# Attention sums taken through DRAM into the row order of the output projection, in an fp32 transformer block on one core

## The chip, the core and the metric

The kernel runs on one core of a Trainium2 chip. Its engines are TensorE (PE in the profile; PEld are its weight loads), VectorE (DVE), ScalarE (ACT), GpSimd (POOL) and SyncE (SP), which here only issues transfers. Each engine works through its own instructions in order; semaphores hold one engine back until another has come far enough. The metric is the time of one execution on the device in microseconds (us). Before the change it is 394.41 us, the median of three runs (393.88 to 394.71).

## The reference

One pre-norm block on x of 2048 tokens by 256, all in fp32: causal attention with 16 heads of 16, then a dense layer with 8 LoRA experts of rank 16, of which each token takes its best two.

```python
h = layernorm(x)
Q, K, V = (heads(h @ W.T) for W in (q_proj, k_proj, v_proj))
p = softmax(causal(Q @ K.T / sqrt(16)))
x = x + merge(p @ V) @ o_proj.T
n = layernorm(x)
logits = n @ gate_w.T + gate_b
best two experts, gates = softmax of their logits
x = x + n @ W.T + b + sum(gate * lora_B[e] @ (lora_A[e] @ n))
```

## The kernel before

The tokens are 16 tiles of 128 and 4 chunks of 512 (4 tiles each). The heads are taken in 4 quads, and two quads are a half (m = 0 or 1). Attention runs with keys on the rows: scores of a block of 128 keys against up to 512 queries go to PSUM (L696), ScalarE takes the exponential of two heads at once (L814), VectorE clears the later keys of diagonal blocks (L1010, the masks), and a product with v_aug adds the block to acc (L713). v_aug holds, for each head, 16 columns of v and 16 of ones, so acc has for each head of a quad 16 rows of numerators and 16 rows that all hold the denominator. When a quad of a chunk is complete, keep_sums copies acc to SBUF (L1015).

The order is set by a table in steps. A step is two units of scores (two exponentials), at most one piece, and the value products of units some steps back. A unit is one bank pair of scores; there are three such pairs, so scores run ahead of the exponentials by little. Chunk c begins at step 0, 10, 36 and 78; the last unit is in step 135. Pieces before attention (turn_x, project_qk, project_v, norms) prepare the next chunk: they stand in steps 0 to 23 and 36 to 49. Pieces after it finish tiles 0 to 11: seven a tile, turn_sums, turn_back, o, turn_y, ffn, turn_gated, lora. All of them use one PSUM bank, aux, so a piece waits until the one before it has been read (bank_read). The four tiles of the last chunk follow when attention is over, in the tail, in an order of their own (TAIL_ORDER).

Per tile, turn_sums (L623) turns the four quads' sums to tokens on the rows, VectorE takes the reciprocal of the 16 denominators (L1020) and multiplies (L1022), turn_back (L630) turns the 256 columns back, VectorE copies them (attn_t, L1027), o multiplies by wo (L637), VectorE adds x (L1033), takes statistics (L1035 to L1040), GpSimd makes the power (L1211), VectorE normalises (yln, L1044). Then turn_y, the copy yT, ffn (L651), the routing (L1055 to L1070), the gates (L1075 to L1089; they wait for GpSimd's exp_gap, L1216), turn_gated (L657), the copy gatedT (L1094), lora (L662), and the result (L1104). The normalisation and the gates are put one step later than their piece, ahead of all else of that step. In the tail ScalarE makes the copies attn_t, yT and gatedT.

SyncE stores the 16-bit parts of q and k of each projected tile to DRAM (L481 to L486) and, when a chunk's four tiles are there, reads them back in the order of the stacks (L455, L464), 16 transfers for a chunk.

## Time and profile before

| | |
|---|---|
| median of 3 runs | 394.41 us |
| profiled execution | 393.18 us, of which the span is 391.4 |
| TensorE busy | 354.2 us (90%) |
| ScalarE busy | 279.5 us (71%) |
| VectorE busy | 209.7 us (54%) |
| GpSimd busy | 47.8 us (12%) |

The span begins with the first instruction and ends with the last; 1.8 us of the execution lie outside it. Busy shares are means over stages that differ, so they don't tell what a stage waits for. A wait in brackets in a timeline is the idle time of the engine before the row, with what ended it.

### The profile page before, as it was taken

What the parts mean: (1) busy time and instruction counts of PE and PEld (TensorE: products, weight loads), DVE (VectorE), ACT (ScalarE), POOL (GpSimd) and SP (SyncE); (2) the same over time, 40 slices, a digit from 0 to 9 for tenths busy, and PEclk for the clock granted to TensorE, in tenths of its full rate; (3) what the DMA queues carried; (4) which work ended last, traced back from release to release, by engine and by line L of the source; (5) the groups of instructions that cost most, each with busy time, mean ns of one, the idle gap of its engine ahead of it and who ended that gap; (6) DMA issues with size and microseconds to landing.
All of it is one profiled execution on the core that took longest, in us unless ns stands there. A gap on an engine that the chain in (4) does not pass through costs nothing.

```text
span 391.4 us, 6977 instructions
## 1 busy us (share of the span) xinstructions
PE 354.2 (90%) x2558; PEld 138.0 (35%) x2558; DVE 209.7 (54%) x711; ACT 279.5 (71%) x317; POOL 47.8 (12%) x75
## 2 busy tenths in 40 slices
PE   8967978899998999999999999998999899799874
PEld 3545524354333444423323233232322323222542
DVE  4555558455755654555447464546346543600785
ACT  2544438677887877888788887888878688799311
POOL 5011000000011100011121111211112111100040
PEclk9997969999999999999999999999999999999997
DMA  6479444222450022271000000000000000000001
GB/s 202 139 224 315 116 131 141 55 55 54 124 148 13 2 54 75 62 214 44 13 2 13 3 13 16 3 13 2 13 16 0 16 0 15 13 2 3 0 3 55
DMA packets 29380, 23.31 MB, mean 60 GB/s; under 512 B 15392, under 2 KB 25888, under 8 KB 29344
## 3 DMA queue, kind: packets, MB, share of 16 engines
q1 hardware_dynamic: 29344, 22.84, 19.8%
q8 instruction: 21, 0.34, 0.4%
q14 instruction: 15, 0.12, 0.1%
HBM read 12.35 MB, written 10.49 MB: 58 GB/s over the span
## 4 chain that ended last, share of the span: by engine, by line
PE 63%; DVE 20%; ACT 7%; issue 6%; POOL 2%; DMA 1%; DVEq 0%; ACTq 0%
PE acc L713 23%; PE scores L696 12%; PE aux L596 7%; ACT probs L814 6%; PE aux L651 5%; PE aux L637 3%; DVE probs L1010 2%; PE aux L662 2%; PE aux L602 2%; PE aux L623 1%; DVE ffn L1055 1%; POOL exp_gap L1216 1%; PE aux L644 1%; DVE gates L1083 1%; DVE parts L954 1%
## 5 line engine op out<-in xcount | busy, mean ns | idle before, releaser
L814 ACT ACTIVATE probs<-scores 128x1024 f32<-128x1024 f32 x272 | 260.2, 1032 | 69.1 <-PE scores L696 59.1
L713 PE MATMUL acc<-probs,v_aug 128*32 128x512 f32 (+3 forms) x1280 | 145.4, 545 | 1.3 <-ACT probs L814 0.9
L696 PE MATMUL scores<-q_stack,k_stack 64*128 64x512 f16 (+3 forms) x640 | 86.5, 352 | 3.7 <-ACT probs L814 2.0
L696 PEld LDWEIGHTS scores<-q_stack,k_stack 64*128 64x128 f16 x640 | 21.1, 94 | 103.6 <-ACT probs L814 80.3
L1010 DVE TENSOR_TENSOR probs<-probs,mask_sb 128x512 f32<-128x512 f32 (+1 forms) x80 | 44.2, 577 | 22.5 <-ACT probs L814 22.0
L713 PEld LDWEIGHTS acc<-probs,v_aug 128*32 128x32 f32 x1280 | 30.8, 110 | 49.8 <-issue 29.7
L596 PE MATMUL aux<-xT,wqkv_sb 128*128 128x128 f32 x192 | 26.3, 294 | 1.0 <-DVE xT L941 1.0
L596 PEld LDWEIGHTS aux<-xT,wqkv_sb 128*128 128x128 f32 x192 | 24.0, 203 | 5.4 <-issue 3.1
L952 DVE CAST parts<-qk 128x512 f16<-128x512 f32 x12 | 5.1, 427 | 36.5 <-ACT qk L806 36.5
L1207 POOL TENSOR_TENSOR rstd<-ve,minus_half 128x1 f32<-128x1 f32 x12 | 7.3, 608 | 101.6 <-DVE ve L932 101.6
L1211 POOL TENSOR_TENSOR rstd<-ve,minus_half 128x1 f32<-128x1 f32 x12 | 6.6, 549 | 103.8 <-DVE ve L1040 103.8
L651 PE MATMUL aux<-wffn_sb,yT 128*128 128x392 f32 x48 | 19.0, 518 | 0.0
L1033 DVE TENSOR_TENSOR y<-aux,x_sb 128x256 f32<-128x256 f32 x12 | 5.1, 424 | 23.9 <-PE aux L637 23.9
L1216 POOL TENSOR_TENSOR exp_gap<-euler,top_gap 128x1 f32<-128x1 f32 x12 | 6.6, 550 | 86.3 <-DVE top_gap L1068 86.3
L1055 DVE COPY ffn<-aux 128x392 f32<-128x392 f32 x12 | 6.8, 567 | 19.0 <-PE aux L651 19.0
L1015 DVE COPY sums<-acc 128x512 f32<-128x512 f32 x16 | 11.0, 686 | 7.0 <-PE acc L713 7.0
L602 PE MATMUL aux<-wqkv_sb,xT 128*128 128x256 f32 x48 | 13.6, 405 | 1.2 <-ACT qk L806 1.0
L1044 DVE TENSOR_SCALAR yln<-y,mv,rstd 128x256 f32<-128x256 f32 x12 | 9.7, 811 | 8.0 <-POOL rstd L1211 8.0
L637 PE MATMUL aux<-wo_sb,attn_t 128*128 128x256 f32 x48 | 13.6, 405 | 0.0
L1104 DVE TENSOR_TENSOR result<-aux,yb 128x256 f32<-128x256 f32 x12 | 5.1, 425 | 14.7 <-PE aux L662 14.7
L806 ACT COPY qk<-aux 128x512 f32<-128x512 f32 x12 | 7.0, 585 | 8.1 <-PE aux L596 5.6
L657 PE MATMUL aux<-ident_sb,gated 128*128 128x128 f32 x12 | 3.9, 327 | 9.0 <-DVE attn_t L1027 8.1
(146 smaller groups left out, 323.0 us busy)
## 6 DMA issues: line engine op xcount, KB each, us to landing
q_stack<-q_dram SPq DMA_DIRECT2D x32, 128.0 KB, 2.8
k_stack<-k_dram SPq DMA_DIRECT2D x32, 128.0 KB, 2.8
qk_dram<-qk SPq DMA_DIRECT2D x12, 256.0 KB, 2.5
x_sb<-x SPq DMA_DIRECT2D x3, 512.0 KB, 6.4
q_dram<-parts SPq DMA_DIRECT2D x12, 128.0 KB, 2.0
k_dram<-parts SPq DMA_DIRECT2D x48, 32.0 KB, 1.9
out<-result SPq DMA_DIRECT2D x12, 128.0 KB, 1.7
qk_dram<-probs SPq DMA_DIRECT2D x4, 256.0 KB, 3.3
```

The source lines that it names most:

```text
L596: m = pe.matmul(aux[:, n * P:(n + 1) * P], wqkv_sb[:, k, col:col + P], xT[:, k, :], start=(k == 0), stop=(k == KH - 1))
L602: m = pe.matmul(aux[:, 0:D], xT[:, k, :], wqkv_sb[:, k, 2 * D:3 * D], start=(k == 0), stop=(k == KH - 1))
L637: m = pe.matmul(w.bank[:, 0:D], w.attn_t[:, k, :], wo_sb[:, k, :], start=(k == 0), stop=(k == KH - 1))
L651: m = pe.matmul(w.bank[:, 0:FFN], w.yT[:, k, :], wffn_sb[:, k, :], start=(k == 0), stop=(k == KH - 1), skip_group_check=True)
L696: m = pe.matmul(scores[u % BANKS][:, j, col:col + n], k_stack[row:row + STACK, kb // TPC, 2 * i + p, kb % TPC * P:(kb % TPC + 1) * P], q_s ...
L713: m = pe.matmul(acc[32 * hp:32 * hp + 32, lo:CHUNK], v_aug[:, kb, QUAD * i + hp, :], probs[:, u % PROBS, hp % 2, col:col + CHUNK - lo], st ...
L814: act.activation(probs[:, u % PROBS], scores[u % BANKS][:], ACT.Exp, scale=EXP_SCALE).then_inc(exp_done, 1)
L1010: dve.tensor_tensor(tile, tile, mask, ALU.min).then_inc(causal_done, 1)
L1015: dve.tensor_copy(sums[:, c % 3, i, :], acc[:]).then_inc(acc_read, 1)
L1044: dve.tensor_scalar(w.yln, w.y, w.mv2[:, 0:1], w.rstd2, ALU.subtract, ALU.mult).then_inc(yln_ready, 1)
L1055: dve.tensor_copy(w.ffn, w.bank[:, 0:FFN]).then_inc(ffn_ready, 1)
L1216: pool.tensor_tensor(w.exp_gap, euler[:], w.top_gap, ALU.pow).then_inc(gap_exp, 1)
```

## The change

Each half of a chunk's sums (two quads, 128 rows by 2 x 512) is stored to DRAM when it is complete, one step later read back with four transfers into `attn`, whose row order is that of the input of o: one plane of numerators, one of denominators, 128 rows by 512 tokens each. wo's rows are permuted on the host to fit. From the fourth step after the store on, VectorE divides one tile (128 x 128) in each of four steps, a reciprocal and a product. o of tiles 0 to 11 takes its input there; turn_sums, turn_back and the copy attn_t go. Their tiles have five pieces. `sums` has one buffer instead of three.

In the tail only the last half (quads 2 and 3 of chunk 3) is still turned, divided and turned back. The first half of the tail's o and the residual x (a product of the identity with x) are put into the banks ahead of the last value products; ScalarE copies the finished sum out (keep_y), and VectorE's addition of x goes.

```diff
-POST_PIECES = ("turn_sums", "turn_back", "o", "turn_y", "ffn", "turn_gated", "lora")
+POST_PIECES = ("o", "turn_y", "ffn", "turn_gated", "lora")
+DIVIDE_LAG = 4
+            for t in range(TPC):
+                at.setdefault(s + DIVIDE_LAG + t, []).append((c, m, t))
...
+            def store_sums(c, m):
+                sp.wait_ge(acc_read, NQUAD * c + 2 * m + 2)
+                sp.dma_start(sums_dram[c, m], sums[:, 2 * m:2 * m + 2, :]).then_inc(sums_out[m], 16)
+
+            def load_sums(c, m):
+                sp.wait_ge(sums_out[m], 16 * (c + 1))
+                if c >= 2:
+                    sp.wait_ge(o_psum, TPC * (c - 1))
+                rows = sums_dram[c, m].rearrange("(h n d) q t -> n q d h t", h=QUAD, n=2)
+                for n in range(2):
+                    for q in range(2):
+                        sp.dma_start(attn[q * P // 2:(q + 1) * P // 2, c % 2, m, n], rows[n, q]).then_inc(sums_in[m], 16)
...
+                    if slot == 0:
+                        for c, m in SUMS_AT.get(s - 1, ()):
+                            load_sums(c, m)
+                        for c, m in SUMS_AT.get(s, ()):
+                            store_sums(c, m)
...
+            def residual(n, w):
+                pe.wait_ge(exp_done, tail_units[n % TPC] + 1)
+                pe.matmul(w.bank[:, 0:D], ident_sb[:], x_sb[:, n, :], start=True, stop=False)
+                pe.wait_ge(divided, divided_upto(NCHUNK - 1, 0, n % TPC))
+                pe.matmul(w.bank[:, 0:D], attn_of(n, 0), wo_sb[:, 0, :], start=False, stop=False)
...
                 piece(s, 0)
+                if s == STEPS - 1:
+                    for t in range(TPC):
+                        run_piece("residual", TILES - TPC + t)
                 for n in GROUPS_AT.get(s, ()):
                     values_of(n)
...
+            def keep_y(g):
+                act.wait_ge(o_psum, g + 1)
+                act.copy(buffers(g).y, buffers(g).bank[:, 0:D]).then_inc(y_kept, 1)
...
             def keep_sums(n):
                 c, i = GROUPS[n].c, GROUPS[n].i
                 dve.wait_ge(pv_done, n + 1)
-                dve.tensor_copy(sums[:, c % 3, i, :], acc[:]).then_inc(acc_read, 1)
+                if c:
+                    dve.wait_ge(sums_out[i // 2], 16 * c)
+                dve.tensor_copy(sums[:, i, :], acc[:]).then_inc(acc_read, 1)
+
+            def divide(c, m, t):
+                n = divided_upto(c, m, t)
+                num, den = (attn[:, c % 2, m, n, t * P:(t + 1) * P] for n in range(2))
+                if t == 0:
+                    dve.wait_ge(sums_in[m], 64 * (c + 1))
+                dve.reciprocal(den, den).then_inc(inverse_ready, 1)
+                dve.wait_ge(inverse_ready, n)
+                dve.tensor_tensor(num, num, den, ALU.mult).then_inc(divided, 1)
...
                 for n in GROUPS_AT.get(s, ()):
                     if GROUPS[n].last:
                         keep_sums(n)
+                for c, m, t in DIVIDE_AT.get(s, ()):
+                    divide(c, m, t)
```

The pairs (chunk, half) are stored in steps 6, 11, 24, 37, 58, 79 and 108 and divided in steps 10 to 13, 15 to 18, 28 to 31, 41 to 44, 62 to 65, 83 to 86 and 112 to 115. The pieces of tiles 0 to 7 end in step 78, those of 8 to 11 stand in steps 87 to 107. Before, pieces went on to step 123.

On VectorE, where the first pair is divided (steps 10 to 13), before:

```order
L932 TENSOR_SCALAR ve<-mv 128x1
L952 CAST parts<-qk 128x4x128
L954 TENSOR_TENSOR parts<-qk,parts 128x4x128
L955 TENSOR_SCALAR clamped<-parts 128x512
L959 TENSOR_TENSOR squares<-clamped 128x4x128
L936 TENSOR_SCALAR xln<-x_sb,mv,rstd 128x256
L1015 COPY sums<-acc 128x512
L965 COPY v_aug<-aux 128x16x16
L941 COPY xT<-aux 128x256
```

and now:

```order
L1015 TENSOR_SCALAR ve<-mv 128x1
L1107 RECIPROCAL held<-held 128x128
L1109 TENSOR_TENSOR held<-held 128x128
L1035 CAST parts<-qk 128x4x128
L1037 TENSOR_TENSOR parts<-qk,parts 128x4x128
L1038 TENSOR_SCALAR clamped<-parts 128x512
L1042 TENSOR_TENSOR squares<-clamped 128x4x128
L1019 TENSOR_SCALAR xln<-x_sb,mv,rstd 128x256
L1100 COPY held<-acc 128x512
L1107 RECIPROCAL held<-held 128x128
L1109 TENSOR_TENSOR held<-held 128x128
L1048 COPY v_aug<-aux 128x16x16
```

A reciprocal and a product (L1107, L1109, both on held) stand between the statistics of a tile and the split of q and k, and again between the copy of the sums and the copy of v.

On TensorE, from the piece ffn of one tile to lora of the same tile, before (L651 ffn, L630 turn_back of the next tile, L657 turn_gated, L662 lora):

```order
L651 MATMUL aux<-wffn_sb,yT 128x392 x2
L713 MATMUL acc<-probs,v_aug 32x512 x8
L696 MATMUL scores<-q_stack,k_stack 128x512 x4
L630 MATMUL aux<-ident_sb,attn_y 128x128 x2
L713 MATMUL acc<-probs,v_aug 32x512 x4
L696 MATMUL scores<-q_stack,k_stack 128x512 x4
L657 MATMUL aux<-ident_sb,gated 128x128
L713 MATMUL acc<-probs,v_aug 32x512 x4
L696 MATMUL scores<-q_stack,k_stack 128x512 x4
L662 MATMUL aux<-lora_b_sb,gatedT 128x256
L713 MATMUL acc<-probs,v_aug 32x512 x4
```

and now (L724 ffn, L710 o of the next tile, L730 turn_gated, L735 lora):

```order
L724 MATMUL aux<-wffn_sb,yT 128x392 x2
L786 MATMUL acc<-probs,v_aug 32x256 x4
L769 MATMUL scores<-q_stack,k_stack 128x512 x4
L710 MATMUL aux<-wo_sb,held 128x256 x2
L769 MATMUL scores<-q_stack,k_stack 128x512 x4
L730 MATMUL aux<-ident_sb,gated 128x128
L786 MATMUL acc<-probs,v_aug 32x512 x8
L769 MATMUL scores<-q_stack,k_stack 128x512 x2
L769 MATMUL scores<-q_stack,k_stack 128x384 x2
L769 MATMUL scores<-q_stack,k_stack 128x128 x2
L735 MATMUL aux<-lora_b_sb,gatedT 128x256
```

o has come to where turn_back stood; lora follows as before.

On TensorE at the end of attention, before (L713 values, L623 turn_sums):

```order
L696 MATMUL scores<-q_stack,k_stack 128x128 x2
L696 MATMUL scores<-q_stack,k_stack 128x256 x4
L713 MATMUL acc<-probs,v_aug 32x512 x8
L713 MATMUL acc<-probs,v_aug 32x384 x4
L713 MATMUL acc<-probs,v_aug 32x128 x4
L713 MATMUL acc<-probs,v_aug 32x256 x4
L623 MATMUL scores<-ident_sb,sums 128x128 x12
L630 MATMUL scores<-ident_sb,k_stack 128x128 x2
```

and now (L685 identity and x, L687 first half of o, L786 values; turn_sums follows):

```order
L786 MATMUL acc<-probs,v_aug 32x512 x8
L685 MATMUL scores<-x_sb,ident_sb 128x256
L687 MATMUL scores<-wo_sb,held 128x256
L685 MATMUL scores<-x_sb,ident_sb 128x256
L687 MATMUL scores<-wo_sb,held 128x256
L685 MATMUL scores<-x_sb,ident_sb 128x256
L687 MATMUL scores<-wo_sb,held 128x256
L685 MATMUL scores<-x_sb,ident_sb 128x256
L687 MATMUL scores<-wo_sb,held 128x256
L786 MATMUL acc<-probs,v_aug 32x384 x4
L786 MATMUL acc<-probs,v_aug 32x128 x4
L786 MATMUL acc<-probs,v_aug 32x256 x4
```

Eight products of 256 columns stand ahead of the last three groups of values; behind them turn_sums has half of its transposes.

## Rows read from the trace of the kernel before

**Rows 1.** Stretches: us, busy (instructions) by engine, PEclk, DMA share, GB/s
```profile
0.00:34.00 34.00, 26.32 (x116) 14.82 (x116) 18.74 (x65) 15.21 (x25) 7.00 (x10) 1.00 0.66 202
34.00:41.00 7.00, 6.05 (x28) 4.26 (x32) 2.92 (x9) 2.25 (x3) 0.92 (x1) 0.51 0.93 292
...
167.90:341.60 173.70, 164.53 (x1197) 51.54 (x1195) 90.53 (x336) 142.00 (x149) 26.20 (x42) 1.00 0.07 21
```

**Rows 2.** Timeline, 202 to 214 us: start us, us, engine, line, operation, tiles
```profile
202.91 0.60 PE L696 MATMUL scores<-q_stack,k_stack 64*128 64x512 f16 x4
...
204.81 0.61 PE L696 MATMUL scores<-q_stack,k_stack 64*128 64x384 f16 x8
...
205.68 0.41 DVE L1027 COPY attn_t<-aux 128x256 f32<-128x256 f32 x1
...
206.15 0.33 PE L657 MATMUL aux<-ident_sb,gated 128*128 128x128 f32 x1 [0.73 <-DVE attn_t L1027]
...
207.41 0.61 PE L696 MATMUL scores<-q_stack,k_stack 64*128 64x256 f16 x6
...
211.28 0.42 DVE L1033 TENSOR_TENSOR y<-aux,x_sb 128x256 f32<-128x256 f32 x1 [1.57 <-PE aux L637]
...
213.24 0.81 DVE L1044 TENSOR_SCALAR yln<-y,mv,rstd 128x256 f32<-128x256 f32 x1 [0.66 <-POOL rstd L1211]
```

**Rows 3.** ScalarE's timeline, 225 to 231 us (three steps: o, turn_sums, turn_y)
```profile
225.50 1.94 ACT L814 ACTIVATE probs<-scores 128x1024 f32<-128x1024 f32 x2 [0.19 <-PE scores L696]
228.09 1.94 ACT L814 ACTIVATE probs<-scores 128x1024 f32<-128x1024 f32 x2 [0.66 <-PE scores L696]
230.22 1.94 ACT L814 ACTIVATE probs<-scores 128x1024 f32<-128x1024 f32 x2 [0.19 <-PE scores L696]
```

**Rows 4.** Chain that ended last, steps without a piece: start us, us
```profile
356.18 1.15 ACT probs L814
...
357.98 1.17 ACT probs L814
```

**Rows 5.** VectorE's groups by shape: xcount, busy us, mean ns
```profile
L1089 DVE TENSOR_TENSOR gated<-ffn,gates 128x128 f32<-128x128 f32 x12 | 3.5, 291 | 0.4
...
L1020 DVE RECIPROCAL inverse<-aux 128x16 f32<-128x16 f32 x12 | 3.0, 248 | 1.8 <-PE aux L623 1.8
...
L1077 DVE RECIPROCAL gate_of<-gate_den 128x1 f32<-128x1 f32 x12 | 2.0, 164 | 0.4
```

**Rows 6.** Timeline, 61 to 75 us, SyncE, VectorE and TensorE
```profile
61.29 1.98 SPq L464 DMA_DIRECT2D k_stack<-k_dram  x4
...
67.03 0.15 DVE L932 TENSOR_SCALAR ve<-mv 128x1 f32<-128x1 f32 x1
...
71.41 0.43 DVE L952 CAST parts<-qk 128x512 f16<-128x512 f32 x1 [4.23 <-ACT qk L806]
...
74.54 0.44 PE L588 MATMUL aux<-ident_sb,xln 128*128 128x128 f32 x2 [1.42 <-DVE v_aug L965]
```

**Rows 7.** DMA issues: count, KB each, median us from issue to landing
```profile
q_stack<-q_dram SPq DMA_DIRECT2D x32, 128.0 KB, 2.8
...
qk_dram<-qk SPq DMA_DIRECT2D x12, 256.0 KB, 2.5
```

**Rows 8.** Timeline, 112 to 149 us, SyncE and VectorE
```profile
111.93 0.42 SPq L464 DMA_DIRECT2D k_stack<-k_dram  x1
...
140.45 0.59 SPq L486 DMA_DIRECT2D qk_dram<-qk  x1
...
148.78 0.42 DVE L941 COPY xT<-aux 128x256 f32<-128x256 f32 x1 [1.34 <-PE aux L588]
```

**Rows 9.** Timeline of the tail, 363 to 371 us
```profile
363.70 1.56 PE L713 MATMUL acc<-probs,v_aug 128*32 128x384 f32 x24 [0.40 <-DVE probs L1010]
...
369.68 1.03 PE L637 MATMUL scores<-wo_sb,k_stack 128*128 128x256 f32 x4
...
370.12 0.43 DVE L1035 BATCH_NORM_STATS2 k_stack<-k_stack 128x6 f32<-128x256 f32 x1
```

More of the change, by code:

```diff
@@ L109, with steps_of_divisions @@
         USED_BY[_u] = _n + 1
-SUMS_STEP = [max(s for s, ns in GROUPS_AT.items() if any(GROUPS[n].c == c for n in ns)) for c in range(NCHUNK)]
+DIVIDE_LAG = 4
+SUMS_AT = {}
+for _s, _ns in GROUPS_AT.items():
+    for _n in _ns:
+        if GROUPS[_n].last and GROUPS[_n].i % 2 == 1 and (GROUPS[_n].c, GROUPS[_n].i) != (NCHUNK - 1, NQUAD - 1):
+            SUMS_AT.setdefault(_s, []).append((GROUPS[_n].c, GROUPS[_n].i // 2))
+def steps_of_divisions():
+    at = {}
+    for s, pairs in SUMS_AT.items():
+        for c, m in pairs:
+            for t in range(TPC):
+                at.setdefault(s + DIVIDE_LAG + t, []).append((c, m, t))
+    return at
+DIVIDE_AT = steps_of_divisions()
+DIVIDED_STEP = [max(s for s, ds in DIVIDE_AT.items() if any(d[0] == c for d in ds)) for c in range(NCHUNK)]
 MASKED = [u for u, x in enumerate(UNITS) if x.masked]
@@ L119 @@
 PRE_PIECES = ("turn_x", "project_qk", "project_v")
-POST_PIECES = ("turn_sums", "turn_back", "o", "turn_y", "ffn", "turn_gated", "lora")
-POST_GAP = {"turn_sums": 1, "turn_back": 1, "o": 2, "turn_y": 1, "ffn": 2, "turn_gated": 1, "lora": 1}
+POST_PIECES = ("o", "turn_y", "ffn", "turn_gated", "lora")
+POST_GAP = {"o": 2, "turn_y": 1, "ffn": 2, "turn_gated": 1, "lora": 1}
 def place_pieces():
@@ L523, in _ @@
             load_rest()
-            for s in range(QK_STEPS):
+            for s in range(STEPS):
                 for slot in range(2):
@@ L1108, in _ @@
                    "norm_k": norm_k}
-            POST = {"turn_sums": divide, "turn_back": store_attn_t, "turn_y": store_yT, "ffn": route_tokens,
+            POST = {"turn_sums": divide_last, "turn_y": store_yT, "ffn": route_tokens,
                     "turn_gated": store_gatedT, "normalise": normalise_y, "gates": gate_inputs}
@@ L1195, in _ @@
             for name, t in TAIL_ORDER:
-                if name not in ("turn_back", "turn_y", "turn_gated"):
+                if name not in ("residual", "turn_back", "turn_y", "turn_gated"):
                     after_piece(name, TILES - TPC + t)
@@ L1264 @@
     order = np.concatenate([(m * (P // DK) + head_of) * DK + row // 4 % DK for m in range(KH)])
+    attn_order = np.concatenate([(m * (P // DK) + row // (P // 2) * QUAD + row % QUAD) * DK + row // QUAD % DK
+                                 for m in range(KH)])
     arrays = {
```

158 lines of the change are left out of this document (96 added, 62 removed).

## The prediction

> **What bounds the kernel now.** I read four views in this order: the table of stretches, the timeline of one stretch in the middle, the chain of waits near the end, and the grouped rows of VectorE. Programs are written in steps. A step on TensorE is two units of scores, at most one "piece" of the projections, LoRA and so on, and the value products. From 167.9 to 341.6 us (steps 50 to 123) TensorE is busy for 164.5 of 173.7 us and ScalarE for 142.0 [rows 1]. Near the end no piece is left, and there ScalarE paces the work: each pair of exponentials starts 1.80 us after the one before (356.18, 357.98) [rows 4]. So 1.80 us is the floor of a step. What TensorE does beyond it is paid for, and a saving on it counts only down to that floor. The 74 steps of [rows 1] at the floor would take 133.2 us, so 40.5 us are lost to pieces and to TensorE's waits.
>
> Three sizes of step follow from [rows 3]. A step with o takes 2.59 us (225.50 to 228.09). One with turn_sums takes 2.13. One with turn_back takes 1.90 (202.91 to 204.81) [rows 2]. The two kinds of piece that go therefore cost 0.33 and 0.10 us a tile over the floor.
>
> The second thing to see is a wait. turn_gated idles 0.73 us, because its bank is released by the copy of attn_t, and VectorE does that copy at 205.68, right behind the gates [rows 2].
>
> **Term A, the pieces (a gain).** Removed per tile: turn_sums and turn_back, 0.33 + 0.10 = 0.43 us; over 12 tiles 5.2 us. The order on TensorE also changes: turn_gated of tile n no longer follows turn_back n+1 but o n+1 (8 of 12 tiles). o takes 2.59 - 1.90 = 0.69 us more, so TensorE comes to turn_gated that much later and waits 0.1 us rather than 0.73. But now a new wait is due. On VectorE o n+1 brings the addition of x, three statistics, and a normalisation that waits for GpSimd's power; all of it stands ahead of the copy of gatedT n. From the addition to the end of that normalisation it takes 213.24 + 0.81 - 211.28 = 2.77 us [rows 2]. If the addition starts at 205.68, where attn_t was copied, gatedT is ready at 208.7. TensorE's scores end at 208.02 (207.41 + 0.61), so lora waits about 0.7 us. Per tile: 0.43 + 0.73 - 0.10 - 0.70 = 0.36 us gained, 4.3 us over 12 tiles. Bounds: with no wait left it is 12 x (0.43 + 0.73) = 13.9 us; with masks between gates and addition (two tiles at least, 0.7 to 1.4 us of masks each, paid at both waits) it is a loss of 1. I take -3.5, the undisturbed pattern less 0.8 for these masks.
>
> **Term B, the divisions on VectorE (a loss).** Before, a tile costs a reciprocal of 16 elements a row (248 ns) and one product. Now there are 28 divisions of 128x128: seven pairs (chunk, half) of four tiles, one in each of four steps in a row. No row shows a reciprocal of 128 elements a row. The nearest two give 164 ns for 1 element and 248 ns for 16, which is 5.6 ns an element, hence 164 + 127 x 5.6 = 875 ns; lower bound, as cheap as the product of the same shape, 291 ns; upper bound, the 15.5 ns an element that 248/16 gives, about 2.0 us [rows 5]. I take 0.88, since the two rows are of the same operation. With 0.29 for the product and the wait between them a division is 1.2 us (0.6 at the low end).
> The transfers: each pair is stored with one transfer of 512 KB and read back with four of 128 KB. A read of 128 KB lands 2.8 us after issue, a store of 256 KB after 2.5 [rows 7]; for 512 KB I take 3.2 (bounds 2.5 and the double, 5.0). SyncE issues a group of four in 1.98 us [rows 6], so the round trip is 0.5 + 3.2 + 2.0 + 2.8 = 8.5 us, where four steps of 1.8 to 2.6 us are allowed (7.2 to 10.4). It starts late where SyncE is busy.
> The Trainium skill ("DMA: Bandwidth & Descriptors", Anatomy of one DMA) puts a transfer at 2.0 us fixed plus its bytes at 436 GB/s: an estimate of 3.2 us for the store and 2.3 for a read; the 2.8 us in the row is longer, and by the rule each round trip would be 0.5 us shorter.
>
> VectorE is in order, so behind a division that waits stand the masks, the copies of xT and v, and the gates; TensorE waits for these in turn. Pair by pair:
> - (0,0), steps 10 to 13: SyncE's loads of the stacks end at 63.27; the store lands near 67, the reads near 72.2. VectorE has had nothing to do since 67.2 and would start the split of q and k at 71.41 [rows 6]; it starts at 73.4 (+2.0). The next division (1.2) stands ahead of the copy of v, for which TensorE already waits 1.42 us at 74.54 [rows 6]. All of it lands there: 3.2 us.
> - (0,1), steps 15 to 18: here data are in time, and each division delays a copy that TensorE needs, xT twice (0.85 and 1.05 us); the delays of v fall where ScalarE paces. 1.9 us.
> - (1,0), steps 28 to 31: SyncE issues the loads of chunk 2 until 112.35 [rows 8]. Store out at 113.0, landed at 116.2, reads landed at about 121.5; VectorE is there at about 118.5, behind gates, masks and yT. It stalls 3 us, then divides, then masks, and only then copies gatedT: lora 0 waits 3.8 us and turn_gated 0 waits 1.9, of which 0.75 were there before. 5.0 us.
> - (1,1), steps 41 to 44: the parts of tile 12 leave until 141.04; reads landed near 150.3. VectorE is free from 147.44 (idle 1.34 before 148.78) [rows 8]; xT is copied at about 151.7 rather than 148.78, and a microsecond of that is cover: 2.0 us, and 1.3 for the two divisions behind it. 3.3 us.
> - (2,0), steps 62 to 65: data in time; one division stands between route and gates, where 0.6 us of waiting for GpSimd hides half. 0.8 us.
> - (2,1) and (3,0): steps 83 to 86 and 112 to 115 have no piece any more; VectorE has room. Nothing.
> Sum: 3.2 + 1.9 + 5.0 + 3.3 + 0.8 = 14.2 us. With divisions of 0.6 us the same sum is 8. With a store of 5.0 us and a reciprocal of 1.3 it is 20, with one of 2.0 near 27.
>
> **Term C, the tail (a loss).** In the last step TensorE is done with its values at 363.30 and idles 0.40 for a mask [rows 9]. There the change puts four residuals: two products of 256 columns each, the size of a piece o, 1.03 us a tile (369.68) [rows 9]. 4 x 1.03 - 0.40 = 3.7 us that the last values, the last copy of sums and all behind them come later. Given back: before the first statistics (370.12 now [rows 9]) half of turn_sums (0.25), a turn (0.13), half of o (0.5), a bit of copying (0.1), together 1.0 us; and the four additions of x leave VectorE (0.42 each), of which GpSimd's pace of 1.3 us a tile lets through about 0.4. From the first gates on, the chain of VectorE is the same. Net +3.7 - 1.4 = +2.3 us. Bounds: 0 if the additions all count, +3.7 if nothing comes back.
>
> **Sum.** -3.5 + 14.2 + 2.3 = +13.0 us on the profiled execution's 393.18, 406.2 us. The median of the runs is 1.2 us above that execution, so I say 406.5.
>
> **Rivals.**
> - Faster: VectorE and the transfers hide all, and the waits at turn_gated vanish without a successor. For it: VectorE is busy for 90.5 of 173.7 us [rows 1]. Against it: order, not load, makes the waits. Gain 13.9 less 2.3 for the tail: 382 us. It decides for "faster" as soon as B is below 1.2 us with A at -3.5. 0.08.
> - Cheap division: the reciprocal goes at the product's speed, only the late data hurt. B = 8: 400 us. Against it: [rows 5]. 0.22.
> - Overload: masks and divisions meet (steps 28 to 31, 56 to 58, 66 to 68), A turns into a loss, the stores of 512 KB take 5 us. B = 18, A = +1: 414 us. 0.15. A part of it could be TensorE's clock; it was granted at 0.51 of full (its level of 1.2 GHz for nearly all of it) from 34 to 41 us, after 34 us in which TensorE was busy for 26.3, and at 1.00 from 167.9 on [rows 1]; one more such stretch beside 3.8 us of idling would cost up to half of 7 us.
> - Break-even: A and B cancel to within a microsecond and the tail is smaller than thought, 394 to 397 us. 0.05.
> - The forecast, 401 to 411 us: 0.50.
> Faster by over 0.2% 0.08, within 0.2% (0.8 us, what a measurement of this kernel can tell from none) 0.02, slower 0.90. The range that leaves out 0.2: 397.5 to 413.5.
>
> **What would show it.** Term A: idle time before lora, ended by gatedT, about 0.75 us in the middle; none above 0.2 before turn_gated there. Term B: reciprocals of 128x128 at 0.88 us; VectorE waiting for a DMA into held at chunks 0 and 1; TensorE waiting for xT, v and gatedT between 66 and 155 us. Term C: 4.1 us of products between the last two groups of values. Wrong would be the forecast if no division waits for its transfer, or if the stretch of free steps (now 37 instead of 14 in the last chunk) starts before 285 us.

## The result and the profile after

| | before | after |
|---|---|---|
| median of 4 runs each | 394.14 us (393.67 to 394.71) | 416.75 us (412.72 to 420.08) |
| profiled execution, span | 393.18, 391.4 us | 417.66, 415.9 us |
| mean granted clock of TensorE | 0.975 | 0.953 |

The ratio is 1.0539, with a 95% interval of 1.0458 to 1.062: slower. The medians are 22.6 us apart. 406.5 was forecast, with a range up to 413.5. The sign was right, the size was not, and the time lies outside the range. Medians here and below are of all runs and ratios of the fast ones alone: the slow ones are 420.08 us of the changed kernel (415.85 is the median of its other three, and against that every gain over it below is 0.9 us smaller), 1743.37 of e2_late_resid, 401.57 of e12_before_pause, and 406.23 and 393.62 of e11_spread_x2, whose other five have a median of 389.54.

First the page of the profile after: engines, the granted clock in 40 slices, the group of the reciprocals, and the two transfers of the sums.

```profile
PE 354.1 (85%) x2482; PEld 133.8 (32%) x2482; DVE 226.5 (54%) x731; ACT 278.9 (67%) x321; POOL 47.1 (11%) x75
...
PEclk9998989698999889999999999999999999989985
...
L1107 DVE RECIPROCAL held<-held 128x128 f32<-128x128 f32 x28 | 26.5, 945 | 26.8 <-DMA held<-sums_dram 26.8
...
sums_dram<-held SPq DMA_DIRECT2D x7, 512.0 KB, 3.2
held<-sums_dram SPq DMA_DIRECT2D x28, 128.0 KB, 2.7
```

ScalarE and TensorE do what they did before; 24 us more of span hold no more work on TensorE. The reciprocals of 128x128 take 945 ns each, and VectorE stands 26.8 us for the sums to land, 14.7 us of it in two waits (7.50 and 7.20, before 275.59 and 341.39) where no piece stands. The clock line has 8 and 9 in slices where it had full speed.

To see where the time went, the step is the best ruler: a step begins with its two exponentials of 128x1024, and both kernels have the same steps, 0 to 135. The table below is worked out from the starts of these exponentials in each trace (us; the tail is from step 135 to the end).

| steps | 0-9 | 10-23 | 24-35 | 36-49 | 50-134 | tail |
|---|---|---|---|---|---|---|
| before | 43.1 | 38.5 | 27.8 | 36.3 | 193.7 | 29.8 |
| after | 41.7 | 49.3 | 39.0 | 38.4 | 192.4 | 32.9 |
| difference | -1.5 | +10.9 | +11.2 | +2.0 | -1.3 | +3.1 |

22 us are lost in 26 steps. They are the steps of the divisions (0,0), (0,1) and (1,0). This is what happens at the first of them, on VectorE (start us, us, engine, line, operation, tiles, [idle before, what ended it]):

```profile
72.20 0.95 DVE L1107 RECIPROCAL held<-held 128x128 f32<-128x128 f32 x1 [6.42 <-DMA held<-sums_dram]
73.18 0.29 DVE L1109 TENSOR_TENSOR held<-held 128x128 f32<-128x128 f32 x1
73.39 0.42 DVE L1035 CAST parts<-qk 128x512 f16<-128x512 f32 x1
...
75.44 0.68 DVE L1100 COPY held<-acc 128x512 f32<-128x512 f32 x1
76.04 0.94 DVE L1107 RECIPROCAL held<-held 128x128 f32<-128x128 f32 x1
...
77.22 0.42 DVE L1048 COPY v_aug<-aux 128x256 f32<-128x256 f32 x1
```

and at the same time on TensorE:

```profile
71.10 0.61 PE L769 MATMUL scores<-q_stack,k_stack 64*128 64x512 f16 x4
77.70 0.69 PE L651 MATMUL aux<-ident_sb,xln 128*128 128x128 f32 x2 [5.99 <-DVE v_aug L1048]
78.32 3.64 PE L786 MATMUL acc<-probs,v_aug 128*32 128x512 f32 x16
```

The same place in the kernel before (two rows of VectorE, one of TensorE):

```profile
64.22 0.69 DVE L1015 COPY sums<-acc 128x512 f32<-128x512 f32 x1 [0.30 <-PE acc L713]
...
74.07 0.41 DVE L965 COPY v_aug<-aux 128x256 f32<-128x256 f32 x1
...
74.91 1.92 PE L713 MATMUL acc<-probs,v_aug 128*32 128x512 f32 x16
```

The division starts at 72.20, and the prediction had the sums landed at 72.2. That agreement is luck. Step 10 begins at 63.82 in this trace and at 65.23 in the one before, so here the changed kernel is 1.41 us ahead, and counted from step 10 the data come 1.4 us later than forecast. The prediction let the store leave when SyncE is free (63.27), but it also has to wait for the copy of acc, which ends at 64.91 in the kernel before (64.22 + 0.69).

VectorE has stood 6.42 us. Then a division, the split of q and k, xln, the copy of acc and a second division all pass ahead of the copy of v_aug at 77.22; before, it stood at 74.07 with the same rows but the two divisions ahead of it. TensorE waits 5.99 us for that copy; before it waited 1.42 [rows 6]. The third of TensorE's rows is the one I had not looked for: the 16 value products behind the wait take 3.64 us. Before, with the clock at full, they take 1.92. The table of stretches says why (columns as in [rows 1]; the first fence is after, the second is before):

```profile
71.00:84.00 13.00, 7.01 (x37) 2.27 (x37) 8.61 (x20) 4.17 (x5) 0.54 (x1) 0.74 0.36 110
97.00:107.00 10.00, 7.75 (x50) 4.74 (x47) 4.21 (x12) 4.91 (x6) 0.54 (x1) 0.83 0.16 42
126.00:148.00 22.00, 13.98 (x80) 4.42 (x82) 13.95 (x42) 9.25 (x10) 2.49 (x4) 0.84 0.10 30
167.90:341.60 173.70, 156.84 (x1152) 49.40 (x1144) 96.65 (x332) 137.30 (x146) 24.18 (x39) 1.00 0.16 50
```

```profile
71.00:84.00 13.00, 11.58 (x90) 5.24 (x94) 7.94 (x22) 9.23 (x11) 0.54 (x1) 1.00 0.21 55
```

From 71 to 84 us the granted clock is 0.74, where it was 1.00. Below full it stands at 0.5, its level of 1.2 GHz. In the trace after there are five such stretches between 70 and 370 us: 76.1 to 82.9, 100.0 to 103.4, 134.1 to 137.5, 144.4 to 147.8 and 362.8 to 366.2. Before has none there. The first four come with or right behind a TensorE wait of 1.2 to 6.0 us: for v_aug at 77.70, xT at 100.33, gatedT at 133.30, and behind the addition of y at 143.90. What brought the fifth I did not find. Nor does every such wait bring one: seven more of 1.25 to 1.97 us (the longest at 213.09 and 240.36) have no low stretch at them. Whom TensorE waits for, in total, times, and the longest:

```profile
PE aux L651 <- DVE v_aug L1048: 11.7, 7, 6.0
PE aux L735 <- DVE gatedT L1191: 9.8, 5, 4.3
PE aux L730 <- DVE y L1129: 6.5, 4, 2.6
PE aux L659 <- DVE xT L1024: 4.5, 6, 1.2
```

In a tile without masks the mechanism of term A is there as forecast. turn_gated waits for nothing, lora waits 0.77 us (0.75 was forecast), and on VectorE the copy of gatedT stands behind the normalisation (TensorE's rows, then VectorE's):

```profile
315.82 0.33 PE L730 MATMUL aux<-ident_sb,gated 128*128 128x128 f32 x1
...
318.46 0.67 PE L735 MATMUL aux<-lora_b_sb,gatedT 128*128 128x256 f32 x2 [0.77 <-DVE gatedT L1191]
...
317.30 0.81 DVE L1141 TENSOR_SCALAR yln<-y,mv,rstd 128x256 f32<-128x256 f32 x1 [0.66 <-POOL rstd L1316]
318.03 0.28 DVE L1191 COPY gatedT<-aux 128x128 f32<-128x128 f32 x1
```

But where VectorE's masks of the diagonal blocks fall between the gates and the addition of x, both waits are there in one tile, 0.98 and 1.97 us:

```profile
209.25 0.33 PE L730 MATMUL aux<-ident_sb,gated 128*128 128x128 f32 x1 [0.98 <-DVE y L1129]
...
213.09 0.67 PE L735 MATMUL aux<-lora_b_sb,gatedT 128*128 128x256 f32 x2 [1.97 <-DVE gatedT L1191]
```

The tail has term C's products, and the statistics behind them:

```profile
384.59 0.70 PE L685 MATMUL scores<-x_sb,ident_sb 128*128 128x256 f32 x2
...
387.72 0.59 PE L687 MATMUL scores<-wo_sb,held 128*128 128x256 f32 x2
388.24 1.50 PE L786 MATMUL acc<-probs,v_aug 128*32 128x384 f32 x24
...
393.63 0.43 DVE L1132 BATCH_NORM_STATS2 k_stack<-k_stack 128x6 f32<-128x256 f32 x1 [0.36 <-ACT k_stack L904]
```

From 384.59 to 388.24 TensorE works through the four residuals (3.65 us). Counted from the start of step 135 the last values start at 5.3 us, and at 2.1 before; the first statistics stand at 10.7, and at 8.5 before [rows 9].

### The profile page after: what moved, and what is told of

It reads as the page before. It is cut to its first block, busy times and chain, and to the rows that moved or that the text cites. A ratio compares the mean times of both kernels' runs of the same rounds, so it can differ in the third digit from the quotient of the medians.

```text
span 415.9 us, 6875 instructions
## 1 busy us (share of the span) xinstructions
PE 354.1 (85%) x2482; PEld 133.8 (32%) x2482; DVE 226.5 (54%) x731; ACT 278.9 (67%) x321; POOL 47.1 (11%) x75
## 4 chain that ended last, share of the span: by engine, by line
PE 38%; DVE 23%; ACT 11%; SPq 9%; issue 9%; DMA 8%; POOL 2%; ACTq 0%; DVEq 0%
PE acc L786 15%; ACT probs L894 10%; PE scores L769 6%; PE aux L724 4%; PE aux L659 4%; DMA sums_dram<-held 3%; DVE probs L1093 3%; DVE held L1107 2%; SPq L500 2%; DMA held<-sums_dram 2%; PE aux L735 2%; SPq L509 2%; SPq L530 2%; DVE parts L1037 1%; SPq L545 1%
## 5 line engine op out<-in xcount | busy, mean ns | idle before, releaser
L786 PE MATMUL acc<-probs,v_aug 128*32 128x512 f32 (+3 forms) x1280 | 149.8, 560 | 0.0
L769 PE MATMUL scores<-q_stack,k_stack 64*128 64x512 f16 (+3 forms) x640 | 89.0, 356 | 7.4 <-ACT probs L894 4.2
L786 PEld LDWEIGHTS acc<-probs,v_aug 128*32 128x32 f32 x1280 | 31.0, 111 | 51.0 <-issue 33.6
L1107 DVE RECIPROCAL held<-held 128x128 f32<-128x128 f32 x28 | 26.5, 945 | 26.8 <-DMA held<-sums_dram 26.8
L659 PEld LDWEIGHTS aux<-xT,wqkv_sb 128*128 128x128 f32 x192 | 24.8, 209 | 9.7 <-DVE xT L1024 7.5
L724 PE MATMUL aux<-wffn_sb,yT 128*128 128x392 f32 x48 | 19.5, 529 | 0.0
L1100 DVE COPY held<-acc 128x512 f32<-128x512 f32 x16 | 11.0, 688 | 15.2 <-PE acc L786 15.2
L735 PE MATMUL aux<-lora_b_sb,gatedT 128*128 128x256 f32 x24 | 8.2, 423 | 9.9 <-DVE gatedT L1191 9.8
L651 PE MATMUL aux<-ident_sb,xln 128*128 128x128 f32 x24 | 5.6, 320 | 12.8 <-DVE v_aug L1048 11.7
L710 PE MATMUL aux<-wo_sb,held 128*128 128x256 f32 x48 | 13.6, 405 | 0.1
```

What stands on the lines that cost most here:

```text
L659: m = pe.matmul(aux[:, n * P:(n + 1) * P], wqkv_sb[:, k, col:col + P], xT[:, k, :], start=(k == 0), stop=(k == KH - 1))
L710: m = pe.matmul(w.bank[:, 0:D], attn_of(n, k), wo_sb[:, k, :], start=(k == 0), stop=(k == KH - 1))
L724: m = pe.matmul(w.bank[:, 0:FFN], w.yT[:, k, :], wffn_sb[:, k, :], start=(k == 0), stop=(k == KH - 1), skip_group_check=True)
L735: pe.matmul(w.bank[:, 0:D], w.gatedT, lora_b_sb[:], start=not w.in_tail, stop=True, skip_group_check=True).then_inc(out_psum, 1)
L769: m = pe.matmul(scores[u % BANKS][:, j, col:col + n], k_stack[row:row + STACK, kb // TPC, 2 * i + p, kb % TPC * P:(kb % TPC + 1) * P], q_s ...
L786: m = pe.matmul(acc[32 * hp:32 * hp + 32, lo:CHUNK], v_aug[:, kb, QUAD * i + hp, :], probs[:, u % PROBS, hp % 2, col:col + CHUNK - lo], st ...
```

## The experiments

Thirteen kernels, each compared with the kernel before on the same chip (medians of 394.0 to 394.6 us there). All edits are made to the changed kernel unless the text says otherwise. Each kernel was profiled once, so the columns by steps are of one trace each.

| label | edit | median us | ratio to before (95%) | steps 10-35 | low clock, steps 10-134 |
|---|---|---|---|---|---|
| before | | 394.1 | 1 | 66.3 | 0 |
| after | | 416.75 | 1.0539 (1.0458-1.062) | 88.3 | 20.4 |
| e3_no_div | no divisions | 396.38 | 1.0072 (1.0039-1.0105) | 68.8 | 6.8 |
| e4_before_div | before + spare divisions | 404.03 | 1.0263 (1.0185-1.034) | 74.7 | 10.2 |
| e7_cheap_division | reciprocal of 0.3 us | 410.23 | 1.042 (1.0373-1.0466) | 79.5 | 17.0 |
| e13_lag7 | divisions 3 steps later | 405.27 | 1.0277 (1.0224-1.0331) | 76.1 | 6.8 |
| e9_keep_busy | TensorE fills four waits | 412.34 | 1.051 (1.0416-1.0603) | 83.4 | 3.4 |
| e1_late_div | divisions late, two a step | 408.39 | 1.0341 (1.0296-1.0387) | 73.8 | 10.2 |
| e2_late_resid | e1, residual last | 409.73 | 1.0382 (1.0337-1.0427) | 72.2 | 10.2 |
| e8_gate_first | gatedT ahead of yln | 411.93 | 1.0454 (1.0402-1.0506) | 89.0 | 17.0 |
| e5_spread | divisions where no piece is | 393.63 | 0.9983 (0.9951-1.0015) | 60.6 | 3.4 |
| e12_before_pause | before, pieces moved | 393.39 | 0.999 (0.9956-1.0023) | 61.0 | 0 |
| e11_spread_x2 | e5 + x on VectorE | 391.65 | 0.9885 (0.9839-0.993) | 60.6 | 3.4 |
| e10_spread_gate | e5 + e8 | 384.56 | 0.9787 (0.9735-0.9838) | 60.6 | 0 |
| **e6_spread_gate_x2** | e5 + e8 + x on VectorE | **382.46** | 0.9707 (0.9675-0.9738) | 60.6 | 0 |

### Are they the divisions, or the transfers?

**e3_no_div**

```diff
-                for c, m, t in DIVIDE_AT.get(s, ()):
-                    divide(c, m, t)
...
-                    pe.wait_ge(divided, divided_upto(n // TPC, KH - 1, n % TPC))
+                    for m in range(KH):
+                        pe.wait_ge(sums_in[m], 64 * (n // TPC + 1))
```

> The changed kernel without its 28 divisions (no reciprocal, no product; o multiplies the undivided sums of the first 12 tiles, so that part of the computation is left out). TensorE, not VectorE, waits for the transfers. SyncE issues every transfer as in the changed kernel. Theory 1: with VectorE free there is no wait before o 0 in step 24, and the time is that of the pieces and the tail, 394.1 - 3.5 + 3 = 394 us, to 398. Rival C (the transfers themselves, or SyncE held in them, delay parts, stacks and results): 404 us or more.

396.38 us: as expected. Steps 10 to 23 take 38.5 us as before, so the stores, the reads and SyncE's queue cost nothing that shows there; 20.4 us hang on VectorE's divisions and on its waits for their data. Steps 24 to 35 take 30.3 us against 27.8 before: that part comes with the new order of the pieces, not with the divisions.

**e4_before_div**, the kernel before with the work of the divisions alone (no transfer, no wait):

```diff
+            def divide_spare(n):
...
+                dve.reciprocal(den, den).then_inc(spare_step, 1)
+                dve.wait_ge(spare_step, 2 * n + 2)
+                dve.tensor_tensor(num, num, den, ALU.mult).then_inc(spare_step, 1)
...
+                if s in DIVIDE_AT:
+                    divide_spare(sorted(DIVIDE_AT).index(s))
```

> The kernel before, with 28 divisions of 128x128 on spare data added on VectorE in the steps in which the change has them; no transfer, no wait for data, pieces and tail as before. Theory 1: what a division costs by its place alone. In chunk 0 and 1 (12 divisions ahead of xT and v) 6 us, in steps 28 to 31 and 62 to 65 about 3, in the last chunk 2 us more than in the changed kernel because pieces stand there; with one or two clock drops 394.1 + 12 = 406 us (403 to 410). Rival D (the waits for transfers are what costs, the work of a division is covered): 394 to 397 us.

404.03 us: as expected. The spare reciprocals have the price of the real ones:

```profile
L1025 DVE RECIPROCAL spare<-spare 128x128 f32<-128x128 f32 x28 | 26.4, 942 | 0.0
```

So the work at these steps is worth 9.5 us (8.4 of it in steps 10 to 35, where two low stretches of the clock come with it), and about as much again, 10.9 of the 20.4 us, is something else.

**e7_cheap_division**, everything in place but the reciprocal's duration:

```diff
-                dve.reciprocal(den, den).then_inc(inverse_ready, 1)
+                dve.tensor_tensor(den, den, den, ALU.is_equal).then_inc(inverse_ready, 1)
```

> The changed kernel with the reciprocal of the sums replaced by an elementwise operation of 0.3 us at the same place (so the division is left out of the result; all waits, transfers and products stay). If the reciprocal's 0.95 us is what costs (28 x 0.65 = 18 us of VectorE), the time falls by 7 to 12, to 405 to 410. If the in-order wait for the transfer is what costs (VectorE and then TensorE stand until the sums have landed, and the clock falls after it), it falls by at most 3, to 413 to 417.

410.23 us, just above the band of the first case and between the two. 28 operations of 305 instead of 945 ns save 18 us of VectorE and 6.5 us of time (the rival Cheap division had put 6.2 between its price and mine). VectorE's stand for the sums stays at 24.8 us:

```profile
L1107 DVE TENSOR_TENSOR held<-held 128x128 f32<-128x128 f32 x28 | 8.5, 305 | 24.8 <-DMA held<-sums_dram 24.8
```

**e13_lag7**, one number:

```diff
-DIVIDE_LAG = 4
+DIVIDE_LAG = 7
```

> The changed kernel with one number changed: divisions start 7 steps behind the last values of their half instead of 4 (so steps 13-16, 18-21, 31-34, 44-47, 65-68, 86-89, 115-118). If VectorE's stand for the transfer in order, and TensorE's behind it, is the larger part of the loss: VectorE's waits for the sums fall from 26.8 us to under 8, 10-24 takes 41 to 46 us instead of 49.3, and the time is 401 to 408. If the work of the divisions in these steps is the larger part and the stands only lie in its slack: 412 or more, with TensorE's waits for xT, v and gatedT in the steps where the divisions now are.

405.27 us, and 43.0 us in steps 10 to 23: as the first case expected. One of its numbers was off. VectorE still stands 14.1 us for the sums and not under 8, but in two waits only, at 265 and 332 us, where no piece of the post-processing stands. The three between 60 and 180 us (6.42, 3.40 and 2.32) are gone. VectorE's wait, and its rows at the first pair:

```profile
DVE held L1107 <- DMA held<-sums_dram: 14.1, 2, 7.6
...
71.18 0.43 DVE L1035 CAST parts<-qk 128x512 f16<-128x512 f32 x1 [4.22 <-ACT qk L886]
...
73.84 0.41 DVE L1048 COPY v_aug<-aux 128x256 f32<-128x256 f32 x1
...
75.87 0.94 DVE L1107 RECIPROCAL held<-held 128x128 f32<-128x128 f32 x1
```

The split of q and k is at 71.18 again, and v is copied at 73.84 with no division ahead of it. The median is 11.5 us lower. I put that down to the in-order stand for the transfer and what follows from it; the edit also moves the divisions past other copies, but the 10.9 us that e4_before_div leaves over say the same by another way. What stays above e3_no_div in steps 10 to 35 is 7.3 us, near the 8.4 that the bare work costs in e4_before_div.

### Is the clock a part of the loss?

**e9_keep_busy**. TensorE does spare products into a free bank of scores before four of its waits; the waits stay.

```diff
+BUSY_AT = {(13, 0): 14, (20, 0): 2, (30, 0): 9, (33, 0): 5}
...
+            def keep_busy(u, times):
+                pe.wait_ge(exp_done, u - BANKS + 1)
+                for _ in range(times):
+                    for j in range(2):
+                        row = STACK * j
+                        pe.matmul(scores[u % BANKS][:, j, :], k_stack[row:row + STACK, 0, 0, 0:P],
+                                  q_stack[row:row + STACK, 1, 0, :], start=True, stop=True, tile_position=(row, 0))
```

> The changed kernel, where TensorE fills four of its stands (before the pieces of steps 13, 20, 30 and 33: turn_x 9, project_qk 11, lora 0, turn_gated 1) with spare products of 64x128 by 64x512 into the next bank of scores (28, 4, 18 and 10 of them), which nobody reads. The stands themselves stay. If the low clock follows a stand and the low clock is a part of the loss, the low stretches at 76, 100, 134 and 144 us go, the work behind them runs as before (step 20 in 4.9 rather than 7.3 us, values x16 in 1.9), and 10-24 and 24-36 take 4 to 8 us less: 408 to 412. If the low clock comes for another reason or costs nothing because another engine sets the pace, the time is 416 to 420.

Timeline of TensorE at the first of them, and the stretches to be set beside those of after:

```profile
72.71 3.20 PE L763 MATMUL scores<-q_stack,k_stack 64*128 64x512 f16 x28 [0.22 <-ACT probs L905]
78.29 0.44 PE L652 MATMUL aux<-ident_sb,xln 128*128 128x128 f32 x2 [2.39 <-DVE v_aug L1059]
78.66 1.92 PE L797 MATMUL acc<-probs,v_aug 128*32 128x512 f32 x16
```

```profile
71.00:84.00 13.00, 10.39 (x82) 4.64 (x82) 8.79 (x21) 6.01 (x7) 0.54 (x1) 1.00 0.32 102
126.00:148.00 22.00, 18.23 (x133) 6.40 (x129) 15.44 (x43) 11.62 (x13) 2.49 (x4) 0.92 0.08 26
```

TensorE still waits until 78.29 for v_aug, but it idles for 2.39 us of that and not 5.99, and the values behind it take 1.92 us, not 3.64. The clock is 1.00 in 71 to 84 us and 0.92 rather than 0.84 in 126 to 148. Steps 10 to 35 take 83.4 rather than 88.3 us: 5.0 us less with added work. No fill outlasts its wait: behind the four of them TensorE still idles 2.39, 0.52, 2.43 and 1.11 us. One low stretch stayed, at 132.0, and step 17, which has no fill, took 4.95 rather than 4.26 us: the kernel had come to the second pair sooner, and VectorE stood 0.59 us for its sums. The median went down by 4.4 us to 412.34, just above the band; the intervals of the two ratios overlap, so the end-to-end figure alone does not show it. The steps do, in one trace of each kernel; the trace of e8_gate_first, which has the same four low stretches as the changed kernel, takes 89.0 us there, near its 88.3.

### Where can the divisions stand?

**e1_late_div**, all eight divisions of a chunk behind it, two a step:

```diff
+DIVIDE_STEPS = {0: (24, 24, 25, 25, 26, 26, 27, 27), 1: (48, 48, 49, 49, 50, 51, 52, 53), ...}
```

> The changed kernel with the divisions of chunks 0 to 2 moved to steps in which their data have long landed and VectorE has room: chunk 0 in steps 24 to 27 (two a step), chunk 1 in 48 to 53, chunk 2 in 83 to 86; all else as changed, transfers and tail too. Theory 1 (divisions that wait for their transfer, or stand ahead of xT, v and gatedT, hold TensorE in chunks 0 and 1, and TensorE's clock falls behind these idle stretches): about 18 of the 22.6 us go, 397 to 401 us. Rival A (the new order of the pieces and the tail cost it): under 4 us go, 412 us or more. Rival B (the clock drops come with the change whatever VectorE does): half goes, 406 us, with as many stretches at 0.5 as the changed kernel has (7 before the tail).

408.39 us: a miss. 8.4 us went, where about 18 were expected. Two divisions in a step of 1.8 us are a queue of their own. VectorE's rows, then TensorE's piece o of tile 1:

```profile
106.43 0.94 DVE L1107 RECIPROCAL held<-held 128x128 f32<-128x128 f32 x1
...
114.75 0.94 DVE L1107 RECIPROCAL held<-held 128x128 f32<-128x128 f32 x1
115.73 0.29 DVE L1109 TENSOR_TENSOR held<-held 128x128 f32<-128x128 f32 x1
115.94 0.75 DVE L1093 TENSOR_TENSOR probs<-probs,mask_sb 128x256 f32<-128x256 f32 x2
...
117.08 1.13 PE L710 MATMUL aux<-wo_sb,held 128*128 128x256 f32 x4 [1.84 <-DVE y L1129]
```

Steps 10 to 23 are as before (38.5 us), so chunk 0's divisions stand for no data any more; but VectorE divides without a gap from 106.43 to 116.02, the masks and the addition wait behind it, and o waits 1.84 us. Steps 24 to 35 take 35.3 us, and 30.3 without divisions.

**e2_late_resid**, the residuals behind the last values:

```diff
+                for n in GROUPS_AT.get(s, ()):
+                    values_of(n)
                 if s == STEPS - 1:
                     for t in range(TPC):
                         run_piece("residual", TILES - TPC + t)
-                for n in GROUPS_AT.get(s, ()):
-                    values_of(n)
```

> As e1, and the four residuals stand behind the last value products instead of ahead of them. Theory 1 takes 3.2 us from the path of the last values and puts 3.5 us of products where TensorE idles 0.9 us for the copy of the sums: 0.5 to 1 us faster than e1. Rival (the residual costs only because the sums come late, and behind them it is hidden by VectorE's chain): 3 us faster than e1.

409.73 us against 408.39: no difference that the runs tell, and neither of the gains. The place of the residuals has no effect that shows.

**e5_spread**, one division a step, in steps from which the pieces were taken:

```diff
+DIVIDE_STEPS = {0: (24, 25, 26, 27, 31, 32, 33, 34), 1: (48, ... 55), 2: (83, ... 90), 3: (124, ... 127)}
+NO_POST = [*range(24, 36), *range(50, 56), *range(83, 91)]
+                if s in NO_POST:
+                    continue
```

> The changed kernel with its 28 divisions one a step where no piece of the post-processing stands (chunk 0 in steps 24 to 27 and 31 to 34, chunk 1 in 48 to 55, chunk 2 in 83 to 90, the first head group of chunk 3 in 124 to 127; the pieces pause in 24 to 35, 50 to 55 and 83 to 90). My theory: the 20 us between the changed kernel (416.8) and the one without divisions (396.4) are VectorE standing for a transfer, TensorE standing for VectorE, and the lower clock that follows each such stand; a division of 1.25 us fits in a step of 1.8 us where VectorE has nothing else. Then 10-24 and 24-36 take within 1.5 us of before, and the time is 394 to 401. Rival: the 35 us of VectorE work is itself the cost, wherever it stands, as 28 spare divisions in before cost 9.5 us: then 403 or more.

393.63 us, a little below the band, and within the interval no different from before. The group of reciprocals is whole and no idle time stands before it:

```profile
L1110 DVE RECIPROCAL held<-held 128x128 f32<-128x128 f32 x28 | 26.4, 944 | 0.0
```

Steps 24 to 35 take 22.1 us, 1.84 each, where the floor of a step is 1.80: 26.4 us of reciprocals cost next to nothing where TensorE wants nothing from VectorE. The 23 us between this kernel and the changed one are places alone, those of the divisions and those of the pieces.

**e12_before_pause** asks if the pause is a gain of its own:

```diff
+NO_POST = range(24, 34)
```

> The kernel before, with nothing changed but the places of its post-processing pieces: none in steps 24 to 33, all ten later. It asks if e6's lead over before comes from the pause alone. A piece costs its work wherever it stands, so the pause gives nothing: 393.5 to 396.5. Rival: chunk 1's steps, whose VectorE has masks and keys to do, pay more for a piece than those of chunk 3: 386 to 391.

393.39 us, 0.999 of before: it isn't. Its steps 24 to 35 take 22.5 instead of 27.8 us and those from 50 on 200.8 instead of 193.7. A pause of 26 steps, as in e5_spread, does not fit into the kernel before: with ten steps of pause its pieces already go on to step 133. The two kinds of piece that the change drops make the room.

### Term A and term C by themselves

**e8_gate_first**: in steps where turn_gated follows o, VectorE copies gatedT before it normalises the next tile.

```diff
+                late = before[0] == "o" and PIECE_AT.get((s, 0), (None,))[0] == "turn_gated"
-                if before[0] in LATER:
+                if before[0] in LATER and not late:
                     after_piece(LATER[before[0]], before[1])
...
+                if late:
+                    after_piece("normalise", before[1])
```

> The changed kernel, with one thing moved: VectorE copies gatedT ahead of the normalising of the next tile. Theory: the 0.77 us that lora stood for gatedT goes in every tile, and nothing new waits; 5 to 12 us faster, 405 to 412. Rival: the normalised tile is late instead and turning it waits as long: 415 to 418.

411.93 us, at the upper edge of the first case, 4.8 us below the changed kernel; the intervals of the two ratios overlap by a little. **e10_spread_gate** has it without the divisions in the way:

> e6_spread_gate_x2 without its edit in the tail: spread divisions, gatedT copied ahead of the normalising, and the changed kernel's tail with TensorE adding x. e5 (393.6) less this is the worth of the gatedT edit, this less e6 (382.5) that of the tail. From the stages of e5 and e6 I expect the gatedT edit to be worth 8 to 9 us (50-135) and the tail 1.5 to 3: 384.0 to 386.0. Rival: the tail's product of x costs nothing or gains (then 382 to 383), as first predicted for term C's counterpart.

384.56 us: as expected, and 9.1 us below e5_spread. Two waits become none (TensorE's rows, then VectorE's; from e6_spread_gate_x2, which has the same order):

```profile
319.67 0.33 PE L733 MATMUL aux<-ident_sb,gated 128*128 128x128 f32 x1
...
321.46 0.70 PE L738 MATMUL aux<-lora_b_sb,gatedT 128*128 128x256 f32 x2
...
320.40 0.28 DVE L1188 COPY gatedT<-aux 128x128 f32<-128x128 f32 x1
321.14 0.81 DVE L1138 TENSOR_SCALAR yln<-y,mv,rstd 128x256 f32<-128x256 f32 x1 [0.47 <-POOL rstd L1316]
```

gatedT is copied at 320.40, 0.74 us ahead of the normalisation, and lora has no idle time before it.

**e11_spread_x2** and **e6_spread_gate_x2**: in the tail x is added by VectorE and o is one piece of four products, as before.

```diff
-                for k in range(1 if w.in_tail else 0, KH):
...
+                for k in range(KH):
...
-                if s == STEPS - 1:
-                    for t in range(TPC):
-                        run_piece("residual", TILES - TPC + t)
...
-                if w.in_tail:
-                    dve.wait_ge(y_kept, n % TPC + 1)
...
+                dve.wait_ge(o_psum, n + 1)
+                dve.tensor_tensor(w.y, w.bank[:, 0:D], x_tile, ALU.add).then_inc(stats2, 1)
```

> e5_spread with only the tail's edit (VectorE adds x there, TensorE does both halves of o after the last values). If the tail's loss is 1.5 to 3 us whatever stands before it: 390.5 to 392.2. If it is nothing: 393 to 394.

> As e5_spread, with two edits more: VectorE copies gatedT ahead of the normalising of the next tile, so that lora no longer waits 0.7 us a tile; and the tail adds x on VectorE as before instead of by TensorE's product with I. Theory: lora's wait goes on some 26 tiles (up to 18 us, of which half was beside steps that wait anyway), and the tail gives back the 3 us it lost: 380 to 392, ahead of both kernels. Rival: the wait only moves to another piece of the same tile (the normalised tile comes later, so turning it waits), and the time is that of e5 less the tail's 3 us, 391 to 398.

382.46 us is 2.1 below e10_spread_gate, as expected. e11_spread_x2 is less certain: 391.65 lies in its band and 2.0 below e5_spread, but the median of 389.54 would be 4.1 below it. The traces agree with each other: in both pairs the tail goes from 31.4 to 29.1 us and steps 10 to 134 stay as they were. e6_spread_gate_x2 is faster than both kernels: 12.1 us ahead of before (ratio 0.9707, 0.9675 to 0.9738) and 34 us ahead of the changed one, with the same arithmetic. How much of the 12.1 us the kernel before would gain from an order of its own, with its wait of 0.73 us at turn_gated taken away, no run here tells.

## Why the prediction was wrong

- **Term B** is the step that failed, in size: 14.2 forecast, 20.4 measured (after less e3_no_div). Its mechanism was right: TensorE waits for v, xT and gatedT behind VectorE's divisions. The table sets its lines beside the traces of the same two kernels (us):

| steps | 10-14 | 15-23 | 24-35 | 36-49 | 50-134 |
|---|---|---|---|---|---|
| forecast for | (0,0): 3.2 | (0,1): 1.9 | (1,0): 5.0 | (1,1): 3.3 | (2,0): 0.8 |
| after less e3_no_div | 7.0 | 3.9 | 8.7 | 2.0 | -1.0 |
| after less e9_keep_busy | 2.6 | 0.8 | 1.6 | -0.1 | 1.7 |

- **What the sum had no line for is the clock.** It stood in the rival Overload, as "one more such stretch". There were five, 20.4 us at 0.5 in steps 10 to 134 by the table of the experiments. In steps 10 to 35 it is worth about the 5.0 us that e9_keep_busy brings back (last row of the table), and one low stretch is still there. That is the larger part of what was missing in term B (6.2 us). I had read one low stretch in [rows 1] and not asked what each of my own TensorE waits would do to the clock behind it. The two longest, of 5.99 and 4.31 us, each carried one. The Trainium skill ("TensorE: Matmul & The Clock Gate", HAM oscillation — how this bites in real kernels) tells of a kernel in which each wait for a transfer between short groups of matmuls brings the lower clock back. This trace agrees at these two waits; of the waits of 1.2 to 2.6 us, two came with a low stretch and others of up to 1.97 us did not.
- **(0,0)**: "All of it lands there: 3.2 us" fails. The wait for v grew by 4.6 us (1.42 to 5.99), and steps 10 to 14 by 7.0. The division that the prediction put ahead of the copy of v is there, with its 1.2 us. The first division delays the split of q and k by 3.4 us counted from step 10 (the split begins 9.57 us behind the start of that step rather than 6.18), not by 2.0: the store waits for the copy of acc, which the sum left out. The lower clock behind the wait adds most of the rest of the 7.0 us.
- **(1,0)**: lora 0 waits 4.31 us (3.8 forecast) and turn_gated 0 waits 1.40 (1.9), but the backlog goes on one tile more, to turn_gated 1, which waits 2.59 us and stood in no line of the sum.
- The single sizes were near: the reciprocal (0.88, measured 0.945), the landing of a read (2.8, measured 2.7) and, as a median, that of the store (3.2, measured 3.2). The slope of 5.6 ns an element came nearer than an estimate of 1.07 us from the repeat count of 8 in the Trainium skill ("VectorE: DVE Perf Modes", First, the fixed hardware budget).
- **Term A**: -3.5 forecast. Without divisions the steps from 24 to 134 take +2.2 us (e3_no_div, 6.8 us of them at a low clock, worth up to 3.4), so the gain was not there. The mechanism was right, with 0.77 for 0.75 us in two tiles. But masks stood between gates and addition in more tiles than the two that I counted: turn_gated waits for y in tiles 1, 3, 5 and 9, and in tiles 3 and 5 lora waits 1.97 us on top. "0.8 for these masks" should have been 3 or more. Of its upper bound, 13.9 us with no wait left, the order of e8 reaches a good part once the divisions are out of the way: steps 24 to 134 of e10_spread_gate take 9.5 us less than before.
- **Term C**: +2.3 forecast. The tail is 3.1 us longer, 6.4 us more of it at the low clock; at nearly like clocks (e5_spread against before, 7.3 and 5.7 us low) it is +1.6. The last values are 3.2 us later, where 3.7 were forecast. That VectorE's additions of x give nearly nothing back was right. Put back to what it was, the tail is 2.3 us shorter (e11_spread_x2 and e6_spread_gate_x2).
- **The rivals**: Overload, 414 us at 0.15, came nearest, for three of its reasons (the clock, divisions beside masks, term A a loss), not for the stores, which took 3.2 us in the median. Break-even and Faster are what the same change gives with its divisions elsewhere (e5_spread) and with the wait at lora gone as well. That e6_spread_gate_x2 has 382.46 and the rival Faster said 382 is luck: the rival kept the loss of the tail, which this kernel takes back.

What remains open: how the 20.4 us split exactly. The runs give the reciprocal's length 6.5, the stand for the transfer 11.5, the clock 4.4 to 5.0 and the bare work 7.3 to 9.5; these overlap, since a stand brings the clock and a shorter reciprocal shortens a backlog.

## What to carry to other kernels

A helper engine at 54% can still stop the leader: what counts is what stands in its queue in the very steps where the leader asks for a copy. Put work with a late input (a transfer's landing) at a step where it has landed, one piece a step, and where the leader asks for nothing; the same 28 divisions stand in a kernel of 416.75 us and in one of 393.63. When a forecast contains a new wait of TensorE of a few microseconds, look what the granted clock did behind such idle stretches elsewhere in the trace, and charge the products behind the longest of them at the lower level.
